# Order of ScalarE's copies in the attention loop, and of gate and w2 loads at the start of the feed-forward part

## What is computed

```python
h = concatenate([patches(x) @ W.T + b, txt], axis=1)              # (8, 548, 192)
n = layernorm(h)
q, k, v = [(n @ w.T).reshape(B, L, 3, 64) for w in (Wq, Wk, Wv)]
s = einsum('blhe,bmhe->bhlm', q, k) / 8 * decay                   # decay: 0 below the diagonal
o = einsum('bhlm,bmhe->blhe', softmax(s), v)
o = (o - mean) / sqrt(var + eps)                                  # mean, var over tokens and a head's features
h = h + (o.reshape(B, L, D) * gn_weight + gn_bias) @ Wo.T
xt = layernorm(h)
comb = top-8 of softmax(xt @ router_w.T), renormalised            # 16 experts, widths 8 x 128 and 8 x 256
out = h + sum_e comb[:, e] * (gelu(xt @ w1_e) @ w2_e)
```

## Time and profile before

| | |
|---|---|
| three timed executions | 762.29, 764.25, 764.98 us (median 764.25) |
| the profiled execution | 762.86 us, of it span 761.1 us |
| TensorE busy | 720.0 us (95%), 4265 matmuls |
| VectorE busy | 574.0 us (75%) |
| ScalarE busy | 469.9 us (62%) |
| GpSimd busy | 158.5 us (21%) |
| chain of waits, by engine | PE 77%, ACT 9%, DVE 7% |

### The profile page before, as it was taken

One profiled execution on the slowest core, in us unless ns is written; L12 is line 12 of the kernel. 1 busy time (PEld: TensorE's weight loads), 2 busy tenths in 40 slices (PEclk: granted clock), 3 DMA queues, 4 the chain that ended last, 5 costly groups with the idle time before them and its releaser, 6 DMA issues.

```text
span 761.1 us, 13144 instructions
## 1 busy us (share of the span) xinstructions
PE 720.0 (95%) x4265; PEld 605.9 (80%) x4265; DVE 574.0 (75%) x1584; ACT 469.9 (62%) x1049; POOL 158.5 (21%) x278
## 2 busy tenths in 40 slices
PE   5978999999998979999999999999999999999996
PEld 4767888888887757888888888888888888888895
DVE  6899888988887657677777777777777777677675
ACT  2678788788787726456456456456456456456453
POOL 3062564574541980000000000000000000000000
PEclk9999999999999989999999999999999999999998
DMA  6700011012112361455255255255265355254142
GB/s 196 210 23 5 20 44 44 3 44 54 55 44 66 125 201 32 113 132 127 77 132 133 71 136 126 74 136 129 70 131 127 76 135 123 71 132 93 47 86 43
DMA packets 120565, 70.14 MB, mean 92 GB/s; under 512 B 82000, under 2 KB 100496, under 8 KB 120496
## 3 DMA queue, kind: packets, MB, share of 16 engines
q1 hardware_dynamic: 120496, 69.31, 36.2%
HBM read 58.65 MB, written 10.63 MB: 91 GB/s over the span
## 4 chain that ended last, share of the span: by engine, by line
PE 77%; ACT 9%; DVE 7%; issue 2%; POOL 1%; DMA 1%; POOLq 1%; DVEq 1%; SPq 1%
PE ps L1425 75%; ACT pt L684 3%; ACT ot L684 2%; ACT pr L764 1%; DVE pr L1117 1%; PE ps L1574 1%; DMA pat<-patches 1%; ACT k_hi L684 1%; DVE sc L1095 1%; DVE xb L1058 1%; ACT xa_hi L684 1%; DVE xa_lo L1058 1%; ACT q L684 0%; DMA gate<-comb_dram 0%; POOL w_lo L641 0%
## 5 line engine op out<-in xcount | busy, mean ns | idle before, releaser
L904 ACT ACTIVATE act<-ps 128x512 f32<-128x512 f32 (+1 forms) x216 | 124.9, 579 | 194.0 <-PE ps L1425 192.7
L1318 DVE TENSOR_TENSOR act<-act,gate 128x512 f32<-128x512 f32 (+1 forms) x216 | 145.5, 674 | 127.3 <-ACT act L904 112.1
L1425 PE MATMUL ps<-x,w_hi 128*128 128x512 f32 (+1 forms) x648 | 215.9, 389 | 0.9 <-ACT act L904 0.8
L1425 PE MATMUL ps<-x,w_lo 128*128 128x512 f32 (+1 forms) x432 | 165.5, 383 | 0.0
L1058 DVE TENSOR_TENSOR act_lo<-act,act_hi 128x512 fp32r<-128x512 f32 (+1 forms) x216 | 145.1, 672 | 0.2
L1425 PEld LDWEIGHTS ps<-x,w_hi 128*128 128x128 f32 x648 | 121.0, 189 | 26.4 <-ACT act L904 2.0
L684 ACT ACTIVATE act_hi<-act 128x512 fp32r<-128x512 f32 (+1 forms) x216 | 130.2, 603 | 9.5 <-DVE act L1318 9.3
L1425 PEld LDWEIGHTS ps<-x,w_lo 128*128 128x128 f32 x432 | 81.5, 189 | 16.4
L1425 PE MATMUL ps<-act_hi,w_hi 128*128 128x512 f32 (+1 forms) x216 | 83.2, 385 | 7.4 <-DVE act_lo L1058 7.3
L536 POOL TENSOR_TENSOR rstdb<-vepsb,neg_half 128x4 f32<-128x4 f32 x9 | 9.7, 1073 | 372.6 <-DVE vepsb L1181 372.6
L1425 PE MATMUL ps<-act_lo,w_hi 128*128 128x512 f32 (+1 forms) x216 | 83.5, 387 | 0.0
(11 more groups left out here) (183 smaller groups left out, 1201.2 us busy)
## 6 DMA issues: line engine op xcount, KB each, us to landing
gate<-comb_dram SPq DMA_DIRECT2D x128, 256.0 KB, 3.6
w_raw<-w SPq DMA_DIRECT2D x16, 384.0 KB, 3.7
h_dram<-h SPq DMA_DIRECT2D x8, 384.0 KB
res<-h_dram SPq DMA_DIRECT2D x8, 384.0 KB, 4.1
rb<-h_dram SPq DMA_DIRECT2D x48, 64.0 KB, 2.6
out<-rb SPq DMA_DIRECT2D x48, 64.0 KB, 1.9
x_dram<-xn_t SPq DMA_DIRECT2D x24, 96.0 KB, 2.4
gate<-comb_dram SPq DMA_DIRECT2D x16, 144.0 KB, 3.0
```

What stands on the lines that cost most here:

```text
L904: a.activation(act[j % 3][:, 0:n], ps[:, up_bank(j), 0:n], ACT.Gelu_apprx_tanh).then_inc(gelu_done, 1)
L1318: dve.tensor_tensor(act[j % 3][:, 0:n], act[j % 3][:, 0:n], gate[e % 4][:, 0:n], ALU.mult).then_inc(gated, 1)
L1425: return pe.matmul(dst, w, x, start=start, stop=stop)
```

## The change

On ScalarE, `x_hi(b + 1, 0)` and `x_hi(b + 1, 1)` now stand ahead of `o_copy(b, 0, ...)`, and `pt_copy(t, 2)` is divided: groups 0 and 1 are copied between `qk_round(b, 2)` and `qk_round(b, 3)`, groups 2 and 3 behind it. TensorE transposes group 0 before it waits for the first `qk_lo`. On SyncE, gates 5 to 7 are issued ahead of w2's part 4 (in place of gate 5 alone), gates 8 and 9 ahead of part 5, gates 10 and 11 ahead of part 6, and part 7 follows part 6. On GpSimd, part 2 is split ahead of `second_rstd(1)` and `norm_second()`. No instruction is added or removed.

```diff
--- before.py
+++ after.py
@@ -468,15 +468,13 @@
             load_w2(2)
             gates(0, 4, 5)
             load_w2(3)
-            gates(0, 5, 6)
+            gates(0, 5, 8)
             load_w2(4)
-            gates(0, 6, 7)
+            gates(0, 8, 10)
             load_w2(5)
-            gates(0, 7, 8)
+            gates(0, 10, 12)
             load_w2(6)
-            gates(0, 8, 9)
             load_w2(7)
-            gates(0, 9, 12)
             store_h(LB - 1)
             gates(0, 12, 15)
             store_h(LB)
@@ -664,11 +662,12 @@
             gn_coefficients(LB - 1)
             split_w2(0)
             split_w2(1)
+            split_w2(2)
             second_rstd(1)
             pool.drain()
             pool.wait_ge(x2t_done, 2)
             norm_second()
-            for p in range(2, W2_PARTS - 1):
+            for p in range(3, W2_PARTS - 1):
                 split_w2(p)
             gn_coefficients(LB)
             split_w2(W2_PARTS - 1)
@@ -844,9 +843,11 @@
                 if tail:
                     o_copy(t, 1, O_BANKS[1])
                 qk_round(b, 2)
+                if tail:
+                    pt_copy(t, 2, (0, 1))
                 qk_round(b, 3)
                 if tail:
-                    pt_copy(t, 2)
+                    pt_copy(t, 2, (2, 3))
                 a.wait_ge(qk_hi, nth(b, 5, 4))
                 copy(k2_hi[0:HD, :], k2_hi[HD:P, :]).then_inc(qk_hi, 1)
                 if not more:
@@ -868,9 +869,9 @@
                 if more:
                     exps(b, 2, (0, 1))
                     pt_copy(b, 1)
-                    o_copy(b, 0, O_BANKS[0])
                     x_hi(b + 1, 0)
                     x_hi(b + 1, 1)
+                    o_copy(b, 0, O_BANKS[0])
                     if tail:
                         gn_totals(t)
                     exps(b, 2, (2, 3, 4))
@@ -1669,8 +1670,9 @@
                 if tail:
                     if t:
                         pe.wait_ge(gn_read, nth(t - 1, 1, 1))
+                    probs_transpose(t, 2, (0,))
                     pe.wait_ge(qk_lo, nth(b, 4, 1))
-                    probs_transpose(t, 2, (0, 1, 2))
+                    probs_transpose(t, 2, (1, 2))
                     pe.wait_ge(qk_lo, nth(b, 4, 2))
                     probs_transpose(t, 2, (3,))
                 scores_pair(b, tail)
```

## The result

The changed kernel took 766.52 us (median of 8 runs, 765.84 to 768.37), the kernel before 762.65 (762.1 to 764.98) beside it: ratio 1.0049, 95% interval 1.0038 to 1.0059. It is slower by some 3.7 us. The forecast was 766.8, which is 3.2 above the 763.6 that it took for the kernel before. The profiled execution took 766.67 us with a span of 764.9, 3.8 above that of before. TensorE is busy 722.3 us (94%), against 720.0.

The account below looks back on a forecast made before the run. A ScalarE/TensorE chain and a nearly full VectorE bound the attention loop; gate 6 stalled TensorE at the feed-forward start. 762.86 + 4.9 (attention) - 1.7 (feed-forward) = 766.1, plus 0.7 for the profiled execution: 766.8 us, range 759.5 to 770.5.

Parts of the forecast that it names:

- The mechanism of the attention part: Attention loop: reordered ScalarE copies make VectorE late at k_lo and den, so VectorE sets the period, 28.2 against 27.33 us.
- The first rival: Attention loop: ScalarE and TensorE bind, VectorE is not late; six bodies gain 0.65 each, 758.0 us; chance 0.12.
- The second rival: Feed-forward start: GpSimd splits at 3.1 us each and the clock stays up, 4.6 us kept, 763.9 us; chance 0.15.
- the third: Rival on the attention part: it costs only 0.3 us a body, 763.5 us in all; chance 0.10.
- the fourth: Rival with both high ends: 1.05 us a body in attention and 4.0 a split on GpSimd, 770.6 us; chance 0.10.
- k_lo becomes +1.48: Third head on VectorE: k_lo waits for k2's rounding, delayed by two copies, and moves from 109.47 to 110.95.
- the 0.85 taken for all: Attention loop: each of bodies 1 to 6 was to take some 0.85 us longer, 5.1 in all.
- +4.9: Whole attention part: 5.1 us lost in six bodies, 0.2 gained in body 7; bounds +1.6 to +6.1.
- -1.7 was forecast: Feed-forward start: removing gate 6's wait gains 8.2 us, but ScalarE's 5.6 us wait for GpSimd's coefficients leaves 1.7.
- the time of GpSimd's program: GpSimd from 256.14: five splits of 3.48, normalisation 5.75 and coefficients 3.47 us, so coefficients are ready at 282.8.
- The 0.7 added for the profiled execution: Final sum: the mean of all four executions, 763.6 us, lies 0.7 above the profiled one, so 0.7 was added.

Follow-up runs that it names:

- edit two: Kernel before with only pt_copy of groups 0 and 1 ahead of k2's rounding and group 0 transposed ahead of q_lo: 764.63 us, ratio 1.0021.
- edits one and two alone: Kernel before with all of the change on ScalarE and TensorE, gates and splits as before: 767.73 us, ratio 1.0057.
- edit one: Kernel before with only the x_hi roundings moved ahead of head 0's output copy on ScalarE: 764.83 us, ratio 1.0019.
- edit two, filled: Edit two alone plus VectorE's gn_stats(t, 0) ahead of the third head's k_lo, against the kernel before: 761.43 us, ratio 0.9972.
- best version: Kernel before with edit three, gn_coefficients(LB) behind part 3's split, edit two, and gn_stats ahead of k_lo: 754.98 us, ratio 0.9887.
- best with edit one: Best version with the x_hi roundings also ahead of head 0's output copy, against the kernel before: 758.22 us, ratio 0.9945.
- Edit three: Kernel before with only SyncE's new gate order and part 2 split ahead of the second normalisation on GpSimd: 762.51 us, ratio 0.9991.
- SyncE's part alone: Kernel before with only SyncE's new gate order; GpSimd still normalises before splitting part 2: 761.18 us, ratio 0.9977.
- edit three with the coefficients earlier: Edit three plus gn_coefficients(LB) on GpSimd moved from behind part 6 to behind part 3's split, against the kernel before: 757.27 us, ratio 0.9919.

## Why the prediction was right, and where its terms were off

**The mechanism of the attention part** was as forecast. The first rival (VectorE not late, 758.0) is out: `k_lo` waits, the first decays have no idle, and filling that wait alone turned edit two by 3.7 us. The second rival (GpSimd keeps pace and the clock stays up) is out by the clock of 0.57, and the third and the fourth (0.3 and 1.05 a body) by the 0.6 to 0.8 that a body cost. `den` stands 107.04 - 102.83 = 4.21 behind the reductions, where 4.20 was worked out (a wait of about 1.1 was forecast; it is 1.24). ScalarE's first rounding waits 0.72 for the reductions.

**Its size was too large.** The step "k_lo becomes +1.48" failed in two of its inputs. TensorE's q and k matmuls start 105.54 - 102.83 = 2.71 behind the reductions, not 104.20 - 101.36 = 2.84; and the two copies delay k's rounding by 0.97 (110.48 to 111.45), not by 1.07, as that row of before counts three instructions which overlap others. So `k_lo` stands 9.27 behind the reductions in place of 9.59, and its wait is 0.60 in place of 0.9. The two inputs make 0.23 of the 0.32. The last four bodies cost 0.60 each by their period. The first two cost 0.8 each, close to the 0.85 taken for all. Six bodies cost 4.1, not 5.1; the end of the part gave 0.5, not 0.2. In sum the traces have +3.5 where +4.9 stood. (Two roundings of the working change nothing: 1.48 - 0.40 is 1.08 and not 1.05, and 292.94 - 291.3 is 1.6 and not 1.7.) The run of edits one and two alone gave 4.3 (3.3 to 5.4).

**What the waits account for** can be read from all the runs at once. The period is the mean of the last four bodies, the waits are all of VectorE's for other engines from 70 to 215 us, about five bodies:

| kernel | waits, us | period, us |
|---|---|---|
| before | 7.4 | 27.30 |
| change | 9.4 | 27.90 |
| edit two | 7.4 | 27.53 |
| edit one | 6.7 | 27.50 |
| edit two, filled | 3.6 | 26.85 |
| best version | 3.6 | 26.85 |
| best with edit one | 6.4 | 27.60 |

Period less a fifth of the waits lies between 25.8 and 26.3 in all seven. That alone does not name the engine that paces the loop, since a period less an engine's idle time is its work, for every engine: TensorE's busy time over the same four bodies also lies between 25.8 and 26.3 a body in all seven. What names VectorE is the pair with edit two, where its order of work alone took the period from 27.53 to 26.85. Nor do the listed waits carry the cost of a single edit: edits one and two alone lengthen the period by 0.2, and their waits are not above those of before. In the body at 101 gaps of 0.10 to 0.14 us, too short to be listed, make up most of the difference: before `xa_lo` and the first decays with edit one, before `xa_lo` and `q` with edit two.

**Edit three** came out at -0.7 us (-1.4 to 0) by its own run, and at +0.4 in the traces, where -1.7 was forecast. The kind of wait, its place and its order of size were right: 6.62 us, 5.6 forecast. The term that failed is the time of GpSimd's program, 26.62 us from part 2's split to the coefficients. It took 287.89 - 259.08 = 28.81. By pieces, measured against forecast: part 2's split 4.27 against 3.48; the normalisation 272.63 - 263.35 = 9.28 against 5.75; parts 3 to 6 12.45 against 13.92, where VectorE stood still beside them for 3.57 us and again from 282.6 on; coefficients 2.81 against 3.47. So the step that failed is the normalisation, 3.5 us too short. (Part 6 came 0.80 behind GpSimd, where 0.2 at most was taken.) The normalisation was taken from a row in which, as it turns out, VectorE had other work. VectorE's timeline beside it, first before, then after:

```profile
259.14 0.78 DVE L1123 BATCH_NORM_STATS2 gst<-ot 64x6 f32<-64x274 f32 x2
259.99 0.27 DVE L1132 BATCH_NORM_AGGREGATE gmv<-gst 128x2 f32<-128x12 f32 x2
```

```profile
267.25 0.83 DVE L1319 TENSOR_TENSOR act<-act,gate 128x512 f32<-128x512 f32 x1
...
268.71 0.84 DVE L1059 TENSOR_TENSOR y<-ot,y 64x548 fp32r<-64x548 f32 x1
...
269.58 0.88 DVE L1319 TENSOR_TENSOR act<-act,gate 128x512 f32<-128x512 f32 x1
```

VectorE was busy in both, 1.88 of 2.10 us before and 6.24 of 6.30 after. The difference is in the kind: statistics with one input from SBUF before, products and subtractions with two inputs after. DMA traffic does not sort the cases: its share was 0.29 beside the 2.07, 0.35 beside the 6.24, and beside 2.92 it was 0.89 in the run with SyncE's part alone and 0.28 in that of edits one and two. No run changed VectorE's neighbours alone, so the cause is read from traces and not shown by an experiment. The prediction applied the slowdown to the splits and left the normalisation at its old duration; moving it by one split had put it beside other instructions. That is also what the lock in the Trainium skill says (SBUF — State Buffer, section SBUF: two separate sides): only VectorE operations with two SBUF inputs, or in a 2-port mode, hold the port pair against a GpSimd operation that reads SBUF. The trace agrees, with 2.07 against 6.24 us for the same four operations. The prediction cited that rule for the splits and took their pace of 3.1 us to be out of reach. That was wrong for parts 3 to 6, which took 12.45 / 4 = 3.11 each, with VectorE at work for 5.5 us of the 12.45; the lateness came from the normalisation.

**The sum** came out so near by luck, because two misses cancel: attention 1.4 us less than forecast, edit three 1.0 to 2.1 less gained. The 0.7 added for the profiled execution was not needed: it lay at 762.86 and the median of the eight runs of before is 762.65, so the 763.6 it started from was 0.9 too high.

What stays open: what edit three is worth alone, and why the first two bodies cost 0.2 more than the others. From the end of the attention part to k = 11 the trace of edit three alone takes 292.56 - 243.38 = 49.18 us, 0.5 more than before, as in the changed kernel. Its span is 0.4 shorter all the same, as its first reductions stand at 45.56 in place of 46.26, where the two kernels do not differ; over all the traces they stand between 45.18 and 46.72. So the timed -0.7 is not seen in the stretch that the edit changes.

## What to carry to other kernels

Where two engines are nearly full in a loop, a shorter wait of the one that ends the chain is worth nothing if the instructions moved ahead delay the other: list the second engine's idle stretches beside every moved step, and give that engine something ready to do where it will wait. In the chain of before VectorE had 7%, and it was still the engine that the change made late. When a stall is removed, ask at once for the next dependency by absolute time and look through the program of the engine that owns it; here its place in GpSimd's order was worth 5.5 us on top of the edit's 0.7. A duration read beside one kind of neighbour doesn't hold when the step moves beside another kind.

## What the runs showed of the hardware

Four GpSimd operations of 128x192 took 2.07, 2.92 or 6.24 us, depending on where they stood; the difference that the traces show is in VectorE's instructions beside them. Single ones took 0.97 to 1.97 us in the changed kernel against 0.50 to 0.60 before, and some of VectorE's took 0.83 to 0.88 beside them, others 0.68. After a stand of TensorE of 5.93 us the granted clock was 0.57 over the next 4.3 us. In the run of edit three with the coefficients earlier, where the longest wait was 1.58, it stayed at 1.00 from 265 to 290. So of the stand's price some is paid after it.
